# An RWKV layer and a cross-attention layer on one core: group norm and gate moved into the scan, mixing products packed, low halves made by GpSimd

## The reference, cut to what matters

```python
# layer 0 (time mixing, then channel mixing); here B=16 sequences, L=128, E=512, H=32 heads of S=16
xn = _ln(x); sx = previous row of xn - xn
xxx = tanh((xn + sx * maa_x) @ maa_w1).reshape(b, l, 5, 1, 32)      # maa_w1: 512 x 160
xxx = matmul(xxx, maa_w2).reshape(b, l, 5, E)                       # five products, 32 x 512 each
x5 = xn[:, :, None] + sx[:, :, None] * (maa_stack + xxx)            # five mixed inputs
w = exp(-exp(time_decay + tanh(x5[1] @ decay_w1) @ decay_w2))
r, k, v = x5[3] @ Wr.T, x5[0] @ Wk.T, x5[2] @ Wv.T;  g = silu(x5[4] @ Wg.T)
# scan over time, per head, state s of 16 x 16:
#   a = k_t v_t;  out_t = r_t (u * a + s);  s = a + w_t * s
att = group norm of out over each head (16 values) * gn_w + gn_b
x = x + att * g @ Wo.T
# then channel mixing (2 norm-mixed products and one more), and layer 1:
# two cross attentions (16 heads of 128) and an MLP of 2048, each with its layer norm and residual
```

## Time and profile before

| | |
|---|---|
| median of three executions | 3397.3 us (3393.8 to 3401.3) |
| the profiled execution | 3398.4 us, span 3396.3 us |
| PE busy | 3121.7 us (92%), x15120 |
| DVE busy | 1942.4 us (57%) |
| ACT busy | 1169.6 us (34%) |
| POOL busy | 396.5 us (12%) |
| mean granted clock of PE | 0.961 |

### The profile page before, as it was taken

One profiled execution on the slowest core, in us unless ns is written; L12 is line 12 of the kernel. 1 busy time (PEld: TensorE's weight loads), 2 busy tenths in 40 slices (PEclk: granted clock), 3 DMA queues, 4 the chain that ended last, 5 costly groups with the idle time before them and its releaser, 6 DMA issues.

```text
span 3396.3 us, 42256 instructions
## 1 busy us (share of the span) xinstructions
PE 3121.7 (92%) x15120; PEld 2408.3 (71%) x15120; DVE 1942.4 (57%) x2861; ACT 1169.6 (34%) x2544; POOL 396.5 (12%) x220
## 2 busy tenths in 40 slices
PE   6878878887885979999999999999999999999899
PEld 3534533533533758888888888787888888888787
DVE  5796696596597754444454444646444464444544
ACT  4203202202202534343444434434444344434332
POOL 0260260160160000000010000101000010000100
PEclk8897997997997989999999999999999999999999
DMA  2001001001002241111111111112111111111011
GB/s 94 25 0 39 0 1 39 0 0 39 0 0 101 74 148 60 50 34 50 52 39 50 34 49 34 56 49 72 50 45 45 50 35 50 34 49 46 19 45 61
DMA packets 52142, 145.75 MB, mean 43 GB/s; under 512 B 4992, under 2 KB 6528, under 8 KB 50912
## 3 DMA queue, kind: packets, MB, share of 16 engines
q1 hardware_dynamic: 52064, 144.77, 12.7%
HBM read 132.17 MB, written 12.58 MB: 43 GB/s over the span
## 4 chain that ended last, share of the span: by engine, by line
PE 60%; DVE 2%; ACT 1%; issue 0%; DMA 0%; ACTq 0%; DVEq 0%
PE ca_ps L59 17%; PE ca_ps L61 17%; PE ca_ps L60 17%; PE ca_ps L1593 3%; PE ca_ps L1577 3%; PE ca_ps L1585 2%; PE ca_ps L1619 1%; DVE ca_stats L67 0%; DVE ca_xres L1354 0%; DVE ca_ctx_lo L1385 0%; DMA ca_xres<-in_ctxT 0%; ACT ca_q L1129 0%; DVE ca_wq_lo L1312 0%; ACT ca_sk L1270 0%; DVE ca_h_lo L1379 0%
## 5 line engine op out<-in xcount | busy, mean ns | idle before, releaser
L1354 DVE TENSOR_TENSOR ca_xres<-ca_xres,ca_ps 128x512 f32<-128x512 f32 x384 | 263.8, 687 | 244.0 <-PE ca_ps L61 239.1
L1141 ACT ACTIVATE ca_pr<-ca_ps,ca_nb 128x129 f32<-128x129 f32 x512 | 181.8, 368 | 510.4 <-DVE ca_nb L1337 510.3
L59 PE MATMUL ca_ps<-ca_h_hi,ca_wq_hi 128*128 128x512 f32 x768 | 313.4, 408 | 11.6 <-ACT ca_q L1129 6.9
L443 DVE TENSOR_TENSOR_SCAN tm_xn<-tm_wd,tm_vb 128x512 f32<-128x512 f32 x256 | 298.4, 1207 | 13.0 <-DVE tm_vb L438 0.5
L61 PE MATMUL ca_ps<-ca_h_hi,ca_wq_lo 128*128 128x512 f32 x768 | 302.5, 394 | 0.0
L60 PE MATMUL ca_ps<-ca_h_lo,ca_wq_hi 128*128 128x512 f32 x768 | 300.4, 391 | 0.0
L59 PE MATMUL ca_ps<-ca_wv_hi,ca_ctx_hi 128*128 128x256 f32 x1024 | 297.7, 291 | 0.0
L61 PE MATMUL ca_ps<-ca_wv_hi,ca_ctx_lo 128*128 128x256 f32 x1024 | 287.3, 281 | 0.0
L60 PE MATMUL ca_ps<-ca_wv_lo,ca_ctx_hi 128*128 128x256 f32 x1024 | 287.1, 280 | 0.0
L59 PE MATMUL ca_ps<-ca_wo_hi,ca_ct_hi 128*128 128x512 f32 x640 | 253.5, 396 | 0.2 <-DVE ca_xres L1354 0.2
L60 PE MATMUL ca_ps<-ca_wo_lo,ca_ct_hi 128*128 128x512 f32 x640 | 252.7, 395 | 0.0
(11 more groups left out here) (237 smaller groups left out, 6615.2 us busy)
## 6 DMA issues: line engine op xcount, KB each, us to landing
ca_sq<-in_wq SPq DMA_DIRECT2D x49, 512.0 KB, 5.4
ca_so<-in_wo SPq DMA_DIRECT2D x48, 512.0 KB, 3.6
ca_sk<-in_wk SPq DMA_DIRECT2D x33, 512.0 KB, 6.4
ca_sv<-in_wv SPq DMA_DIRECT2D x32, 512.0 KB, 3.7
ca_bvr<-in_bvb SPq DMA_DIRECT2D x32, 256.0 KB, 3.9
tm_xq<-in_x SPq DMA_DIRECT2D x5, 1024.0 KB, 7.6
tm_gg<-in_l0w SPq DMA_DIRECT2D x4, 1024.0 KB, 4.9
tm_rr<-in_x SPq DMA_DIRECT2D x4, 1024.0 KB, 5.1
```

What stands on the lines that cost most here:

```text
L59: pe.matmul(out, lhs[0], rhs[0], start=first, stop=False)
L443: v.tensor_tensor_scan(state[t % 2][:, d, :], wd[:, g].rearrange("p b t -> p (b t)"), pair[:, d, :], 0.0, ALU.mult, ALU.add).then_inc(scan ...
L1141: ins = act.activation(pr[hd][:, b, :], ps[:, BANK_SC + b // 2, o:o + KW], ACT.Exp, bias=nbs[hd][:, b:b + 1], scale=SCALE, accum_out=sms[h ...
L1354: v.tensor_tensor(xres[U.h][:, U.quad * 4 + b, :], xres[U.h][:, U.quad * 4 + b, :], ps[:, BANK_O + b % 2, :], ALU.add).then_inc(o_out, 1)
```

## The change

In `time_mix`:
- `x_lo` of all six inputs (24 a quad) is made by POOL (`lo`), no more by DVE.
- The mixing products for r, k, v and g become one fp32r product with K=96: high weights with high and low h5, low weights with high h5. For that ACT copies the high half of h5, DVE subtracts the low one, and POOL starts 12 DMAs a quad, each 32 partitions x 512 within on-chip memory, that stack the three parts into `packed`. They stand in POOL's list ahead of `lo` for j = 1. The mixing product for w stays as it was.
- The gate's stage (j = 5) is taken out from ahead of the scan. Its 12 matmuls for each output chunk f run in two halves inside the scan, those of f = 3 behind it.
- Group norm and gate of chunks 0 to 2 run inside the scan, eight steps behind their sums: head centring is one product (I - mean), variance and unpacking go chunk by chunk in bank `pj0`, gn_w is folded into ACT's evacuation, gn_b and gate are one DVE instruction. Chunk 3 follows the scan, interleaved with the output product, which now goes to `vb`.
- The bonus sums and the splits of v for chunks 1 to 3 move into the first steps of the scan.
- x is loaded by sequence during the scan; the layer norm statistics of the next quad move up in the tail, and the last pass makes no norm. Several tiles share memory (`h5_split` with `rr`, `v_hi` with `xq`, `packed` with `vv`).
- The passes are now q = 0, a loop over 1 and 2, and q = 3; on POOL all four are written out.

In `cross_attend`, the second query product of a pair, where it goes into BANK_K, no longer waits for the evacuation of the first.

```diff
+        xq, v_hi = shared("xq", [P, 4, E], "v_hi", [P, EC, QT])
...
+        rr, h5_split = shared("rr", [P, EC, QT], "h5_split", [P, 4, QT])
+        kk, kk_fr = shared("kk", [P, EC, 4, L + 1], "y_hi", [P, EC, 4, L + 1])
+        vv_at = nc.sbuf_base
+        vv, vv_fr = shared("vv", [P, EC, 4, L + 1], "y_lo", [P, EC, 4, L + 1])
+        packed = nc.alloc_sbuf_tensor_at("tm_packed", [96, 4, QT], FR, offset=vv_at)
+        gg, v_lo = shared("gg", [P, EC, QT], "v_lo", [P, EC, QT])
...
+            def load_x(q, b):
+                sp.dma_start(xq[:, b, :], io["x"][bass.ds(q * 4 + b, 1)].rearrange("a t e -> (a t) e")).then_inc(x_in[b // 3], 16)
...
+                if not last:
+                    for b in range(4):
+                        sp.wait_ge(vb_full, q * STEPS + 8 * (b + 1))
+                        load_x(q + 1, b)
...
+            def pack(s, m):
+                hi, lo = (h5_split[32 * m:32 * m + 32, 0, :], h5_split[32 * m:32 * m + 32, 1, :]) if m < 4 else (
+                    h5_split[0:LORA, 2, :], h5_split[0:LORA, 3, :])
+                for k, part in enumerate((hi, hi, lo)):
+                    gp.dma_start(packed[32 * k:32 * k + 32, s, :], part).then_inc(pack_in[min(s, 1)], 16)
+            def lo(q, j):
+                for c in range(EC):
+                    gp.wait_ge(hi_ready, q * (4 * J) + (4 * j + c + 1))
+                    gp.tensor_tensor(x_lo[:, c, :], xf[:, c, :], x_hi[:, c, :], ALU.subtract).then_inc(split_ready, 1)
+            lo(0, 0)
+            gp.wait_ge(w_ready, 4)
             gp.memset(wd[:], 0.0).then_inc(ready, 1)
+            for q in range(NQ):
+                if q > 0:
+                    lo(q, 0)
+                gp.wait_ge(hl_hi, q * 2 + 1)
+                gp.wait_ge(hl_lo, q * 2 + 1)
+                for s in range(3):
+                    pack(s, MIX[s + 2])
+                gp.wait_ge(hl_hi, q * 2 + 2)
+                gp.wait_ge(hl_lo, q * 2 + 2)
+                pack(3, MIX[5])
+                for j in range(1, J - 1):
+                    lo(q, j)
+                gp.wait_ge(mx_full, q * 20 + 20)
+                gp.memset(vv[:, :, :, 0:1], 0.0).then_inc(pad_ready, 1)
+                gp.wait_ge(w_hi_ready, 6)
+                gp.memset(kk[:, :, :, 0:1], 1.0).then_inc(pad_ready, 1)
+                lo(q, J - 1)
...
+                def gate(f):
+                    act.wait_ge(g_full, q * 4 + (f + 1))
+                    act.activation(gg[:, f, :], pj[1][:], ACT.Silu).then_inc(g_ready, 1)
+                def square(f):
+                    act.wait_ge(cent_full, q * 4 + (f + 1))
+                    act.activation(ew[:], mx[f % 2][:], ACT.Square).then_inc(cent_out, 1)
+                    w = VEC["gn_w"] + f
+                    act.activation(vv[:, f, :, 1:L + 1], quad3(mx[f % 2][:]), ACT.Identity, scale=vec[:, w:w + 1]).then_inc(cent_out, 1)
+                def deviation(f):
+                    act.wait_ge(var_full, q * 4 + (f + 1))
+                    act.activation(grs[:], pj[0][:, 0:P], ACT.Sqrt, bias=eps[:]).then_inc(gstd_ready, 1)
+                def gated_hi(f):
+                    act.wait_ge(y_ready, q * 8 + (2 * f + 2))
+                    act.activation(y_hi[:, f], vv[:, f, :, 1:L + 1], ACT.Copy).then_inc(y_hi_ready, 1)
...
+                act.activation(h5_split[:, 0, :], h5[:], ACT.Copy).then_inc(hl_hi, 1)
+                act.wait_ge(lora_out, q * 3 + 2)
+                act.activation(h5_split[0:LORA, 2, :], h4, ACT.Copy).then_inc(hl_hi, 1)
+                if first:
+                    act.wait_ge(spread_in, 32)
+                    act.activation(lora2p[:], raw_lora2, ACT.Copy).then_inc(w_hi_ready, 1)
...
+                    for f in range(3):
+                        if t == 8 * f + 11:
+                            gate(f)
+                        if t == 8 * f + 12:
+                            square(f)
+                        if t == 8 * f + 14:
+                            deviation(f)
+                        if t == 8 * f + 17:
+                            gated_hi(f)
+                gated_hi(2)
+                gate(3)
+                square(3)
+                if not last:
+                    roots(q + 1)
+                deviation(3)
...
+                v.tensor_tensor(h5_split[:, 1, :], h5[:], h5_split[:, 0, :], ALU.subtract).then_inc(hl_lo, 1)
+                v.wait_ge(hl_hi, q * 2 + 2)
+                v.tensor_tensor(h5_split[0:LORA, 3, :], h4, h5_split[0:LORA, 2, :], ALU.subtract).then_inc(hl_lo, 1)
+                if first:
+                    v.wait_ge(w_hi_ready, 4)
+                    v.tensor_tensor(lora2p[32:64], raw_lora2[32:64], lora2p[32:64], ALU.subtract).then_inc(w_ready, 1)
...
+                def gated(f):
+                    v.wait_ge(unpacked, q * 4 + (f + 1))
+                    v.wait_ge(cent_out, q * 8 + (2 * f + 2))
+                    v.tensor_tensor(vv[:, f, :, 1:L + 1], vv[:, f, :, 1:L + 1], quad3(pj[0][:]), ALU.mult).then_inc(y_ready, 1)
+                    b_ = VEC["gn_b"] + f
+                    v.wait_ge(g_ready, q * 4 + (f + 1))
+                    v.wait_ge(y_ready, q * 8 + (2 * f + 1))
+                    v.scalar_tensor_tensor(out=vv[:, f, :, 1:L + 1], in0=vv[:, f, :, 1:L + 1], scalar=vec[:, b_:b_ + 1],
+                                           in1=quad3(gg[:, f, :]), op0=ALU.add, op1=ALU.mult).then_inc(y_ready, 1)
+                def gated_lo(f):
+                    v.wait_ge(y_hi_ready, q * 4 + (f + 1))
+                    v.tensor_tensor(y_lo[:, f], vv[:, f, :, 1:L + 1], y_hi[:, f], ALU.subtract).then_inc(y_split_ready, 1)
...
+                    if t == 0:
+                        bonus(0)
+                    if 1 <= t <= 3:
+                        value_lo(t)
+                    if t in (2, 3):
+                        bonus(t - 1)
+                    if t == 5:
+                        bonus(3)
+                    for f in range(3):
+                        if t == 8 * f + 10:
+                            add_bonus(f)
+                        if t == 8 * f + 14:
+                            inverse(f)
+                        if t == 8 * f + 15:
+                            gated(f)
+                        if t == 8 * f + 17:
+                            gated_lo(f)
...
+                gated_lo(2)
                 add_bonus(3)
+                if not last:
+                    norm_stats(q + 1, 3)
+                    norm_aggregate(q + 1)
+                inverse(3)
+                gated(3)
+                gated_lo(3)
+                if not last:
+                    norm_apply(q + 1)
...
+                    if j == 1:
+                        lhs, rhs = lora2[32:64, c * P:(c + 1) * P], h5[32:64, :]
                     else:
+                        if c == 0 and j == 2:
+                            pe.wait_ge(pack_in[0], q * 48 + 48)
+                        elif c == 0:
+                            pe.wait_ge(pack_in[1], q * 144 + 144)
+                        lhs, rhs = lora2p[:, j - 2, c * P:(c + 1) * P], packed[:, j - 2, :]
                     pe.matmul(mx[n % 2][:], lhs, rhs, start=True, stop=True).then_inc(mx_full, 1)
...
+                for t in range(STEPS):
                     spread(t + 2)
                     if t >= 1:
                         accumulate(t - 1)
+                    if t == 2:
+                        bonus(3)
+                    for f in range(3):
+                        if t in (8 * f + 8, 8 * f + 9):
+                            gate(f, t - (8 * f + 8))
+                        if t == 8 * f + 10:
+                            centred(f)
+                        if t == 8 * f + 12:
+                            variance(f)
+                        if t == 8 * f + 14:
+                            unpacks(f)
+                gate(3, 0)
+                gate(3, 1)
+                accumulate(STEPS - 1)
+                if first:
+                    pe.wait_ge(w_ready, 8)
+                pe.wait_ge(scanned, q * (3 * STEPS) + 3 * STEPS)
+                output(0)
+                centred(3)
+                output(1)
+                variance(3)
+                output(2)
+                unpacks(3)
+                output(3)
...
-                pe.wait_ge(q_out, C.n * 2 + hd)
+                pe.wait_ge(q_out, C.n * 2 + (hd if bank == BANK_Q else 0))
```

More of the change, by code:

```diff
@@ L211, in quad @@
[L211 to L220 removed]
+            sp.dma_start(raw_spread, io["spread_v"]).then_inc(spread_in, 16)
@@ L472, in quad @@
-                    if b < 3:
-                        link(ins)
-                ins.then_inc(quad_done, 1)
-                assert steps.n == DVE_STEPS
-            v.wait_ge(ready, 4)
-            norm(0)
+                    v.tensor_tensor(rr[:, b, :], rr[:, b, :], vb[:, b, :], ALU.add).then_inc(res_added, 1)
+            v.memset(std[:], 1.0)
+            for b in range(4):
+                norm_stats(0, b)
+            norm_aggregate(0)
             v.wait_ge(w_hi_ready, 2)
@@ L523, in stage @@
```

(55 more changed lines are left out.)

544 lines of the change are left out of this document (261 added, 283 removed).

## The result

The changed kernel takes 3279.0 us in the median (3277.4 to 3279.5, four runs) beside 3395.5 us for the kernel before on the same chip (3388.6 to 3401.3, four runs): ratio 0.9657, 95% interval 0.9638 to 0.9676. That is some 117 us faster. The forecast was 3331 us with a range down to 3290: the sign was right, the size too small, and the range missed the time. In the profiled executions the span fell from 3396.3 to 3275.6 us, 120.7 us. One later execution of the changed kernel, at a granted clock of 0.76, took 3760 us; it is in no median here.

The account below looks back on a forecast made before the run. PE bounds cross_attend; time_mix is a relay with PE, DVE and chains limiting in turn. 69.6 - 57.2 + 48.0 + 6 = 66.4 us off 3398.4 gives 3332, 1.1 lower for the median: 3331; range 3290 to 3385.

Parts of the forecast that it names:

- The price of a DMA issue on GpSimd: Ahead of the r stage: 1.0 us per POOL issue, twelve a pass; that stretch loses 3.4 us.
- Rival 2: Ahead of the r stage: POOL issues cost SP's shortest, 0.43 us; 27 us less, 3304; chance 0.15.
- The stretch r to v: r, k, v products ahead of the scan: ten mixing products each 0.77 us shorter, 51.2 becomes 43.5 us.
- End of v to K: End of the v stage to the first multiplication by k: 8.0 becomes 4.7 us, 3.3 less.
- T to K: First token-shift instruction to first multiplication by k: 104.5 becomes 86.0 us; 69.6 less over all passes.
- Scan: First multiplication by k to last scan's end: work moved onto DVE adds 14.3 us a pass, 57.2 in all.
- Tail: S, the last scan's end, to T, the next pass's first token-shift instruction: 48.0 us shorter in all.
- cross_attend: Cross-attention: PE's waits in eight places for the first query's evacuation vanish, 6 us less (bounds 0 and 6.9).
- 1: Ahead of the r stage: the 12 DMAs hold POOL longer; 3427 us at 3 us an issue, or 3518; chance 0.08.
- rival 3: Scan and token shifts: no exclusion between DVE and POOL, 14 us and 4 us less, 3313; chance 0.10.
- the first form of 4: Scan: PE drops to the low clock and becomes the limit, 228 us more, 3559; chance 0.02.
- the milder form of 4: Scan: each of 12 half gates runs 0.9 us late on PE, 10 us more, 3341; chance 0.05.

Follow-up runs that it names:

- e6: Changed kernel plus twelve more same-size DMAs per pass issued by GpSimd behind the packing DMAs, into an unread tile: 3301.1 us, 0.9720 of the kernel before.
- e4: Changed kernel with the mixing products of mixes 2 to 4 in fp32 and unpacked, as before the change: 3316.0 us, 0.9755 of the kernel before.
- e2: Changed kernel with the low halves of mixes 1 to 5 back on DVE: 3301.2 us, 0.9716 of the kernel before.
- e7: e2 with the last low half of mix 5 moved behind the four r*u*k products and first split of v: 3288.8 us, 0.9683 of the kernel before.

## Why the prediction was wrong

- **The price of a DMA issue on GpSimd.** This is the step that failed most: "I take 1.0, the median of the row whose form is nearest". It was 0.51, and twelve issues held GpSimd for 5.91 us, not 12.0. The r stage came 6.3, 6.4 and 6.2 us sooner than forecast in passes 1 to 3: 6.1 from the hold and 1.0 because the first issue started at T + 14.3 and not T + 15.3, less 0.8 that the chain behind the first `lo` took longer. e6 shows that a us of hold counts 0.8 to 0.9 us on the path. The rows offered 0.43 to 2.39, and the form with a run-time address was the wrong neighbour. Rival 2 (issues at 0.43) had the right mechanism and still fell short at 3304, because the next terms were missing.
- **The stretch r to v**, "51.2 becomes 43.5", became 40.3. Of the 3.2 us, 2.2 are the first chunk: I carried over into the new kernel the time PE spent at the low clock at the start of the old r stage (5.0 instead of 2.8 us) without noticing that it was in the 51.2. In e4, with the products unpacked, it is back (1.5 to 2.5 us); but the level of the clock there differs from pass to pass in several kernels, so its going away was no sure effect of the change. The rest is the mixing product, 0.87 us less each ((10.9 - 2.2)/10) instead of 0.77; e4 has 0.84.
- **End of v to K**, 8.0 becomes 4.7, was 3.6. I had the r*u*k products stretch beside the `lo`, and they do (4.80 us for four), but all save the last 1.3 us of it lies under the v stage. That is not free: PE then waits 2.02 us for the split of v, which stands behind them. e2 and e7 show what moving the low halves does here: the last one leaves DVE's list, and nothing useful queues behind a wait for ACT.
- **One pass taken for three.** I scaled pass 1 of the kernel before (104.5 us from T to K). Passes 2 and 3 have 110.5 and 103.3. The kernel before varies here (100.0 to 110.5 over two profiles of the same `time_mix`), with granted clocks ahead of the r stage between 0.59 and 0.68; the changed one does not (75.2 to 75.5). This is 4.8 of the 44.4 us.
- Passes 1 to 3 together: 18.9 ahead of the r stage, 9.6 from r to v, 3.3 from v to K. Pass 0 adds 7.8, in which the issues held GpSimd for 6.0 us instead of 12.0 as well; the rest of it I did not split. With the 4.8 the sum is 44.4.
- **Scan**: right, 54.5 for 57.2, and the 1.8 us turn at the gate instruction is there (2.45 against 0.73). **Tail**: right, 48.3 for 48.0; next T at S + 25.2, 26.3 and 25.3, residual sums at S + 23.6.
- **cross_attend**: the wait vanished as said. The size is 4 to 8 us by the timings, around the forecast's 6, and 9.9 by the mean of all traces; the first pair of profiles showed 12.4.
- **Rivals.** 1 and 3 did not happen, nor did the first form of 4: the longest issue is 0.68 us, the turn is real, and DVE stays the limit of the scan (126.4 of 127.5 us). Of the milder form of 4 the waits of 0.3 to 0.5 us in passes 0 and 3 are at most a trace. The Trainium skill gives in "SBUF — State Buffer", section "A bandwidth-pool intuition that's wrong (but worth ruling out)", about 620 ns for a DMA from GpSimd alone and about 3100 ns beside a VectorE copy, without saying which part of a DMA that is. Read as the price of an issue, as the prediction did, the first is above the 0.51 measured here, and no run here comes near the second.

The range failed at its lower end, which left 41 us, for rival 2 and a part of rival 3. Rival 3 did not occur. The shorter hold is some 24 us over four passes (6.1 each), and r to v, v to K, the other passes of the kernel before and `cross_attend`, for which the range had next to nothing, all fell to the same side.
